# Attention weights times values with the values as TensorE's weights, in four column groups, and a way through HBM to put the result in order

## The chip, the cores and the metric

The kernel runs on one core of one Trainium2 chip. The metric is the device time of one execution in microseconds. A core has TensorE (matmuls, which write to PSUM), VectorE, ScalarE, GpSimd and SyncE; each runs its own queue in order and waits on semaphores. The profile names them PE (and PEld for TensorE's weight loads), DVE, ACT, POOL and SP.

## The reference

The input x has 16 sequences of 256 tokens of 128 numbers, all in fp32. It is one layer with an attention branch and a branch of experts on the same normalised input:

```python
xn = layernorm(x)
x = x + attn(xn) + ffn(xn)
# attn: h = layernorm(xn)*g1+b1; 16 query heads, 4 key/value heads, head size 8, rope
scores = where((col <= row) & (row - col < 32), q @ k.T / sqrt(8), -1e9)
out = softmax(scores) @ v                # the part that is changed
x1 = xn + out @ Wo + bo
attn = x1 + gelu(layernorm(x1) @ Wf1 + bf1) @ Wf2 + bf2
# ffn: 8 experts of 448 hidden units, the best two for each of the 4096 tokens
y = sum_e gate_e * (silu(x @ w1_e.T) * (x @ w3_e.T)) @ w2_e.T
```

## The kernel before

**Stages.** First x is normalised, q, k, v and the gate scores are computed for all tokens, and each (token, expert) pair gets a slot, so that 72 tiles of 128 slots each hold rows of a single expert. Then come 12 steps (k = 0 to 11), each with 6 expert tiles and parts of the attention of four neighbouring batches. Steps 3 to 10 are two-step bodies of a hardware loop; all others are written out. Steps 12 to 18 have no expert tiles: there the attention of the last batches is finished, and the feed-forward part of the attention branch (`up`, `down`), the sum of the experts' results and the stores of the output run. This is called the tail.

**An expert tile.** POOL gathers 128 rows of xn by an indirect DMA. TensorE transposes them (`transpose_xs`), VectorE copies them out (`take_xsT`), TensorE makes 7 products (`up_products`), ScalarE applies silu, VectorE multiplies (`gated`), TensorE makes 4 products (`down_product`), ScalarE takes the result out and POOL scatters it to HBM. A `down_product` waits for the copy `take_xsT` of the next tile, since both use one PSUM bank. SP loads the weights of a tile (448 KB) three tiles ahead, as soon as the products of the tile that used the buffer are done.

**Attention of batch b.** A batch has 256 queries in 8 blocks of 32. In its scores, partitions hold (key/value head, query in the block) and columns (head of the group, key). Because the window is 32 wide, the 32 columns of a query's own block and those of the block before can share one set of 32: for each query a key position is either in its own block or in the older one. `older_scores` and `own_scores` make both, `shift` takes one or the other and subtracts the maximum, `exps` takes exponentials and `weights_T` transposes. So `pT[:, n]` holds (head, key) by (g, query) for block n, and `pO[:, n]` the part of it that belongs to the own block. `vbd` holds the values of a block, block-diagonal over the four key/value heads, with four columns of ones behind (36 columns), and `dv` the difference to the block before. The result is the sum of pT with the older values and pO with the difference.

**The product that is changed** is `attend`, in four quarters of two blocks. `pT[:, n]` or `pO[:, n]` (128 columns) are the weights and `vbd` or `dv` (36 columns) move; block 0 has one product, each other block two, 15 in all. The result of block n stands in `turn_bank` with (g, query) in partitions and (head, d) and the four sums in columns. `norm` takes reciprocals of 32 sums, multiplies 256 columns, and one VectorE transpose in blocks of 32x32 makes `outT`, whose rows are features and columns tokens, as `project` (the product with Wo) needs it.

**Order of work around it.** Step k has, on TensorE: own scores of k, `heads` of k+1, tile, older scores of k, tile, own scores of k, tile, older scores, `transpose_h2` of k-3, tile (with quarter 0 of `attend(k-1)` ahead of the down product and quarter 1 behind it), tile (`project(k-2)` and quarter 2 ahead of the down product, quarter 3 behind it). In the tail no expert products stand between the quarters. `heads(b)` writes into `turn_bank`, and waits for `pv_normed` of batch b-3. VectorE does `norm(k-1)` as the last thing of step k, behind `residual(k-2)`. SP's queue has only weight loads in the steps, and in the tail loads of the experts' results and stores of the output, each behind waits for VectorE.

Of the kernel before, what the change touches and what calls it, by code (L numbers as in the profile page):

```python
# [22 lines left out]
P = 128  # L23
B, T, D = 16, 256, 128
NTOK = B * T
# [47 lines left out]
def layer(nc, x, wqkv, bqkv, wo, bo, g1, b1, g2, b2, wf1, bf1, wf2, bf2, gate, w13, w2,  # L73
          ident, cosf, sinf, older, newer, qmask, vmask, tri, rev, tilegrid, places, column, row, xn, ys, out):
# [4 lines left out]
    with ctx:  # L79
        def sb(name, shape, dt=F32):  # L80
            return ctx.enter_context(nc.sbuf_tensor(name, shape, dt))[:]

        def sem(name):
            return ctx.enter_context(nc.semaphore(name))
# [50 lines left out]
        def table(*shape):  # L135
# [103 lines left out]
        exp_ready, pT_ready, pv_psum, rsum_ready, pv_normed = (sem("exp_ready"), sem("pT_ready"), sem("pv_psum"),  # L239
                                                               sem("rsum_ready"), sem("pv_normed"))  # L240
# [34 lines left out]


# [21 lines left out]
        def _(sp):  # L298
# [160 lines left out]
        def _(dve):  # L459
# [245 lines left out]
            def norm(b):  # L705
                dve.wait_ge(pv_psum, b + 1)
                pv = turn_bank[:, 0:NBLK * VW].rearrange("p (n c) -> p n c", c=VW)
                nc.vector.reciprocal(rsum, pv[:, :, NKV * HD:VW]).then_inc(rsum_ready, 1)
                dve.wait_ge(rsum_ready, b + 1)
                nc.vector.tensor_tensor(  # L710
                    on.rearrange("p (n h d) -> p n h d", h=NKV, d=HD),
                    pv[:, :, 0:NKV * HD].rearrange("p n (h d) -> p n h d", d=HD),
                    bc(rsum.rearrange("p n (h a) -> p n h a", a=1), [P, NBLK, NKV, HD]), ALU.mult).then_inc(pv_normed, 1)
                dve.wait_ge(pv_normed, b + 1)
                nc.vector.transpose(outT, on).then_inc(outT_ready, 1)
# [311 lines left out]
        def _(pe):  # L1027
# [92 lines left out]
            def attend(b, p, quarter, h2T_out):  # L1120
                if quarter == 0:
                    pe.wait_ge(pO_ready, b + 1)
                    pe.wait_ge(dv_ready, b + 1)
                    if some(h2T_out):
                        pe.wait_ge(h2T_ready, h2T_out)
                for n in range(quarter * NBLK // 4, (quarter + 1) * NBLK // 4):
                    to = turn_bank[:, n * VW:(n + 1) * VW]
                    if n > 0:
                        nc.tensor.matmul(to, pT[:, n].rearrange("p g q -> p (g q)"), vbd[:, p, n, :], start=True, stop=False)  # L1129
                    last = nc.tensor.matmul(to, pO[:, n].rearrange("p g q -> p (g q)"), dv[:, p, n, :], start=(n == 0), stop=True)  # L1130
# [254 lines left out]
```

## Time and profile before

| | |
|---|---|
| median of 3 runs | 502.0 us (501.33 to 503.25) |
| profiled execution | 500.98 us, span 498.8 us |
| TensorE matmul busy | 437.2 us (88% of the span) |
| TensorE weight loads busy | 396.8 us (80%) |
| VectorE busy | 375.2 us (75%) |
| ScalarE busy | 254.9 us (51%) |
| GpSimd busy | 224.5 us (45%) |
| mean granted TensorE clock | 0.94 |
| moved by DMA | 57.21 MB |

The span runs from the first to the last instruction that the profiler recorded. Matmuls are pipelined and their ends are modelled, so the busy time of TensorE says less than the distance between the starts of neighbouring records. A share over the whole span is a mean over stages with different limits.

### The profile page before, as it was taken

What the parts mean: (1) busy time and instruction counts of PE and PEld (TensorE: products, weight loads), DVE (VectorE), ACT (ScalarE), POOL (GpSimd) and SP (SyncE); (2) the same over time, 40 slices, a digit from 0 to 9 for tenths busy, and PEclk for the clock granted to TensorE, in tenths of its full rate; (3) what the DMA queues carried; (4) which work ended last, traced back from release to release, by engine and by line L of the source; (5) the groups of instructions that cost most, each with busy time, mean ns of one, the idle gap of its engine ahead of it and who ended that gap; (6) DMA issues with size and microseconds to landing.
All of it is one profiled execution on the core that took longest, in us unless ns stands there. A gap on an engine that the chain in (4) does not pass through costs nothing. (4 is left out here: it accounts for less than half of the span.)

```text
span 498.8 us, 11145 instructions
## 1 busy us (share of the span) xinstructions
PE 437.2 (88%) x3310; PEld 396.8 (80%) x3311; DVE 375.2 (75%) x1010; ACT 254.9 (51%) x536; POOL 224.5 (45%) x252
## 2 busy tenths in 40 slices
PE   2943939879999999999999999989999999997996
PEld 2832539768989898989898989989999787785873
DVE  7947555857777777777777777777877979849874
ACT  2584244454645455555546465545545737553432
POOL 3630032546464656464646465555553841312320
PEclk9985558989999999999999999999999999999799
DMA  8950123424444545343444444433450600222211
GB/s 230 260 197 0 45 87 128 148 92 145 137 145 137 149 122 156 113 144 126 147 137 138 142 142 128 143 111 132 142 143 8 166 5 1 68 60 64 64 43 42
DMA packets 38033, 57.21 MB, mean 115 GB/s; under 512 B 6238, under 2 KB 25442, under 8 KB 37872
## 3 DMA queue, kind: packets, MB, share of 16 engines
q1 hardware_dynamic: 32528, 47.66, 31.5%
q0 software_dynamic: 4608, 8.93, 5.8%
q8 instruction: 18, 0.29, 0.2%
q10 hardware_dynamic: 864, 0.20, 0.2%
q14 instruction: 15, 0.12, 0.1%
HBM read 48.38 MB, written 8.91 MB: 115 GB/s over the span
## 5 line engine op out<-in xcount | busy, mean ns | idle before, releaser
L1166 PE MATMUL bank<-xsT,w_sb 128*128 128x128 f32 x1008 | 132.2, 284 | 16.1 <-DVE inter L761 10.8
L1166 PEld LDWEIGHTS bank<-xsT,w_sb 128*128 128x128 f32 x1008 | 121.0, 195 | 21.9 <-issue 18.4
L409 POOL DMA_INDIRECT scratch_ys<-ysb,pair x72 | 77.1, 1071 | 124.0 <-ACT ysb L953 114.5
L402 POOL DMA_INDIRECT xsb<-scratch_xn,token x72 | 73.8, 1026 | 59.7 <-DVE token L593 35.4
L1179 PE MATMUL bank<-w_sb,inter 128*128 x576 | 79.6, 281 | 4.1 <-issue 3.3
L1179 PEld LDWEIGHTS bank<-w_sb,inter 128*128 128x128 f32 x576 | 69.9, 191 | 7.6 <-issue 7.3
L953 ACT ACTIVATE ysb<-bank 128x128 f32<-128x128 f32 x72 | 19.8, 275 | 82.7 <-PE bank L1179 79.6
L759 DVE TENSOR_TENSOR inter<-bank,act 64x128 f32<-64x128 f32 x72 | 21.2, 295 | 38.2 <-ACT act L947 32.5
L1130 PE MATMUL bank<-dv,pO 128*128 128x36 f32 x256 | 49.3, 276 | 0.6 <-ACT h2T_sb L907 0.6
L1130 PEld LDWEIGHTS bank<-dv,pO 128*128 128x128 f32 x256 | 39.6, 194 | 2.7 <-issue 2.7
L761 DVE TENSOR_TENSOR inter<-bank,act 128x384 f32<-128x384 f32 x72 | 40.2, 558 | 1.0
L1129 PE MATMUL bank<-vbd,pT 128*128 128x36 f32 x224 | 40.8, 266 | 0.0
L750 DVE COPY xsT<-bank 128x128 f32<-128x128 f32 x72 | 20.7, 288 | 25.4 <-PE bank L1155 23.6
L946 ACT ACTIVATE act<-bank 64x128 f32<-64x128 f32 x72 | 19.4, 269 | 33.2 <-PE bank L1166 19.7
L947 ACT ACTIVATE act<-bank 128x384 f32<-128x384 f32 x72 | 35.4, 491 | 0.8
L930 ACT ACTIVATE S<-bank 128x512 f32<-128x512 f32 x32 | 19.5, 610 | 31.3 <-DVE pT L695 25.3
L1095 PE MATMUL bank<-kT,qbd 128*128 128x128 f32 x256 | 34.8, 280 | 0.7 <-ACT S L930 0.7
L1193 PE MATMUL bank<-h2T_sb,wf_sb 128*128 128x512 f32 x64 | 32.4, 631 | 2.3 <-ACT h2T_sb L907 1.3
L1129 PEld LDWEIGHTS bank<-vbd,pT 128*128 128x128 f32 x224 | 34.1, 192 | 0.0
L1108 PE MATMUL bank<-kT,qbd 128*128 128x128 f32 x224 | 31.5, 281 | 2.8 <-DVE S L682 2.8
L1204 PE MATMUL bank<-wf_sb,gT_sb 128*128 128x128 f32 x256 | 33.3, 293 | 0.8 <-ACT gT_sb L962 0.8
L1095 PEld LDWEIGHTS bank<-kT,qbd 128*128 128x128 f32 x256 | 32.1, 196 | 2.0 <-issue 1.1
(154 smaller groups left out, 810.0 us busy)
## 6 DMA issues: line engine op xcount, KB each, us to landing
w_sb<-in_w SPq DMA_DIRECT2D x72, 448.0 KB
w_sb<-scratch_ys SPq DMA_DIRECT2D x16, 256.0 KB, 3.3
scratch_xn<-xn_sb SPq DMA_DIRECT2D x8, 256.0 KB, 4.4
w_sb<-in_w SPq DMA_DIRECT2D x1, 2048.0 KB, 9.0
out_dram<-x_sb SPq DMA_DIRECT2D x8, 256.0 KB, 2.8
xsb<-scratch_xn,token POOLq DMA_INDIRECT x72
scratch_ys<-ysb,pair POOLq DMA_INDIRECT x72
x_sb<-in_x SPq DMA_DIRECT2D x3, 256.0 KB, 3.7
```

The costliest lines, as they stand in the source:

```text
L402: nc.gpsimd.indirect_dma_start(xsb[:, j % 3, :], None, xn, bass.IndirectOffsetOnAxis(ap=token[:, j:j + 1], axis=0)).then_inc(slots_in[j % ...
L409: nc.gpsimd.indirect_dma_start(ys, bass.IndirectOffsetOnAxis(ap=pair[:, j:j + 1], axis=0), ysb[:, j % 3, :], None, bounds_check=2 * NTOK - ...
L761: nc.vector.tensor_tensor(inter[:, p, 0:FULL], h3_bank[:, 0:FULL], act1[:, p, 0:FULL], ALU.mult).then_inc(inter_ready, 1)
L947: nc.scalar.activation(act1[:, p, 0:FULL], h1_bank[:, 0:FULL], ACT.Silu).then_inc(silu_ready, 1)
L1095: last = nc.tensor.matmul(bank[0][:, i * GW:(i + 1) * GW], qbd[:, p, n].rearrange("p h q -> p (h q)"), kT[:, p, :, (n + 1) * WIN:(n + 2) * ...
L1108: last = nc.tensor.matmul(bank[1][:, i * GW:(i + 1) * GW], qbd[:, p, n].rearrange("p h q -> p (h q)"), kT[:, p, :, n * WIN:(n + 1) * WIN], ...
L1129: nc.tensor.matmul(to, pT[:, n].rearrange("p g q -> p (g q)"), vbd[:, p, n, :], start=True, stop=False)
L1130: last = nc.tensor.matmul(to, pO[:, n].rearrange("p g q -> p (g q)"), dv[:, p, n, :], start=(n == 0), stop=True)
L1166: last = nc.tensor.matmul(to[:, c % EC * P:(c % EC + 1) * P], w13_sb[:, i % 3, c * P:(c + 1) * P], xsT[:, p, :], start=True, stop=True)
L1179: last = nc.tensor.matmul(y_bank[:, 0:D], inter[:, p, c * P:(c + 1) * P], w2_sb[:, ds(at + c * P, P)], start=(c == 0), stop=(c == EC - 1))
L1193: nc.tensor.matmul(bank[4 + c % 2], wf1_sb[:, c * P:(c + 1) * P], h2T_sb[:, i * 512:(i + 1) * 512], start=True, stop=True).then_inc(up_psu ...
L1204: last = nc.tensor.matmul(bank[6 + i % 2][:, t * D:(t + 1) * D], gT[i % 4][:, c, t * P:(t + 1) * P], wf2_sb[:, c, :], start=(c == 0), stop ...
```

## The change

For batches 0 to 14 the values become the weights (32 columns: four heads of 8), and the attention weights move (128 columns). The 32 result rows of block n = 4a + c go to partitions 32c to 32c+31, so that blocks c = 0 to 3 use the four column groups of the array. Quarters 0 and 2 make 8 such products (pT with the older values, then pO with the difference), quarters 1 and 3 make 4 products with `vmask_sb` as weights, which give the sums of the exponentials on the same rows as the results. In all there are 24 products for the 15 of before.

`norm` then takes reciprocals of 256 columns and multiplies; there is no transpose. The result `on` has (c, head, d) in partitions and (a, g, query) in columns. SP stores it to a scratch tensor in HBM and loads it again with four DMAs, one for each g, into `outT`, in runs of 32 numbers. These stand in SP's queue among the weight loads of step k = b+2 and, for the last batches, among the loads and stores of the tail. Batch 15 keeps the products, the narrow reciprocal and the transpose.

```diff
-        rsum = sb("rsum", [P, NBLK, NKV])
+        rsum = sb("rsum", [P, T])
...
+        def is_plain(b):
+            return isinstance(b, int) and b == B - 1
...
-            with sp.Fori(1, SLOT_TILES // 3) as n:
-                for p in range(3):
-                    load_weights(n, p)
+            def store_values(b):
+
+                sp.wait_ge(pv_normed, b + 1)
+                sp.dma_start(turned, on).then_inc(out_stored, 16)
+
+            def load_heads(b):
+
+                sp.wait_ge(out_stored, 16 * (b + 1))
+                for g in range(G):
+                    sp.dma_start(outT[g * 32:(g + 1) * 32, :].rearrange("x (a c q) -> x a c q", a=2, c=4),
+                                 turned.rearrange("(c x) (a g q) -> g x a c q", c=4, a=2, g=G)[g]).then_inc(outT_ready, 16)
+
+            def step(m, tiles=TILES):
+                for i in range(tiles):
+                    load_weights(2 * m + i // 3 + 1, i % 3)
+                    if i == 1 and exists(m - 2):
+                        store_values(m - 2)
+                    if i == 2 and exists(m - 2):
+                        load_heads(m - 2)
...
+            step(MSTEPS - 1, 3)
+            store_values(MSTEPS - 2)
+            load_heads(MSTEPS - 2)
...
+            regroup_first = {0: MSTEPS - 1, 1: MSTEPS, 2: MSTEPS + 1, 4: MSTEPS + 2}
             for i in range(GROUPS_A):
+                if i in regroup_first:
+                    store_values(regroup_first[i])
+                    load_heads(regroup_first[i])
                 sp.wait_ge(second_added, i + 1)
...
+                else:
+                    nc.vector.reciprocal(rsum, turn_bank[:, T:2 * T]).then_inc(rsum_ready, 1)
+                    dve.wait_ge(rsum_ready, b + 1)
+                    nc.vector.tensor_tensor(on, turn_bank[:, 0:T], rsum, ALU.mult).then_inc(pv_normed, 1)
...
+                else:
+                    a, total = quarter // 2, quarter % 2
+                    for i in range(1 if total else 2):
+                        for c in range(4):
+                            n = 4 * a + c
+                            to = turn_bank[32 * c:32 * c + 32, total * T + a * P:total * T + (a + 1) * P]
+                            weights = (pO if i else pT)[:, n].rearrange("p g q -> p (g q)")
+                            values = vmask_sb[:, 0:NKV * HD] if total else (dv if i else vbd)[:, p, n, 0:NKV * HD]
+                            last = nc.tensor.matmul(to, values, weights, start=(i == 0), stop=(i == 1 or total == 1))
...
-                pe.wait_ge(outT_ready, b + 1)
+                if is_plain(b):
+                    pe.wait_ge(last_turned, 1)
+                else:
+                    pe.wait_ge(outT_ready, 16 * G * (b + 1))
```

## Rows read from the trace of the kernel before

**Rows 1.** The page: busy time, share of the span, instructions of an engine

```profile
PE 437.2 (88%) x3310; PEld 396.8 (80%) x3311; DVE 375.2 (75%) x1010; ACT 254.9 (51%) x536; POOL 224.5 (45%) x252
```

**Rows 2.** Busy time in the window of one step; TensorE's longest wait, whole run

```profile
core 0: us, PE busy (x) PEld busy (x) DVE busy (x) ACT busy (x) POOL busy (x), PEclk, DMA share, GB/s
204.28:230.10 25.82, 24.75 (x214) 23.99 (x213) 19.97 (x52) 14.13 (x32) 14.72 (x16) 1.00 0.45 136
...
PE bank L1166 <- DVE inter L761: 10.8, 18, 2.3
```

**Rows 3.** TensorE's groups by shape: count, busy us, mean ns, idle before

```profile
L1129 PE MATMUL bank<-vbd,pT 128*128 128x36 f32 x224 | 40.8, 266 | 0.0
L1095 PE MATMUL bank<-kT,qbd 128*128 128x128 f32 x256 | 34.8, 280 | 0.7 <-ACT S L930 0.7
```

**Rows 4.** Timeline of TensorE in a step: start, length, records

```profile
222.62 0.31 PE L1130 MATMUL bank<-dv,pO 128*128 128x36 f32 x2
...
223.50 1.15 PE L1179 MATMUL bank<-w_sb,inter 128*128 x8
224.49 0.31 PE L1129 MATMUL bank<-vbd,pT 128*128 128x36 f32 x2
...
225.30 1.81 PE L1166 MATMUL bank<-xsT,w_sb 128*128 128x128 f32 x14
...
230.10 1.81 PE L1166 MATMUL bank<-xsT,w_sb 128*128 128x128 f32 x14
...
231.85 1.06 PE L1095 MATMUL bank<-kT,qbd 128*128 128x128 f32 x8
232.74 0.27 PE L1081 MATMUL bank<-ident_sb,qr 128*128 128x128 f32 x1
```

**Rows 5.** Timeline of VectorE in the same step and after it

```profile
223.08 0.28 DVE L750 COPY xsT<-bank 128x128 f32<-128x128 f32 x1
...
230.30 0.36 DVE L708 RECIPROCAL rsum<-bank 128x32 f32<-128x32 f32 x1 [0.17 <-PE bank L1130]
...
230.69 0.42 DVE L710 TENSOR_TENSOR on<-bank,rsum 128x256 f32<-128x256 f32 x1
...
232.05 0.29 DVE L750 COPY xsT<-bank 128x128 f32<-128x128 f32 x1 [0.45 <-PE bank L1155]
...
233.59 0.29 DVE L759 TENSOR_TENSOR inter<-bank,act 64x128 f32<-64x128 f32 x1 [1.25 <-ACT act L947]
```

**Rows 6.** VectorE's groups by shape, the whole run

```profile
L715 DVE STREAM_TRANSPOSE outT<-on 128x256 f32<-128x256 f32 x16 | 7.1, 445 | 0.5
...
L624 DVE RECIPROCAL mult<-mult 128x64 f32<-128x64 f32 x1 | 0.6, 553 | 0.0
```

**Rows 7.** Timeline of TensorE in the tail; brackets: idle before, and what ended it

```profile
415.25 1.16 PE L1108 MATMUL bank<-kT,qbd 128*128 128x128 f32 x8 [0.88 <-DVE S L682]
...
458.23 1.16 PE L1108 MATMUL bank<-kT,qbd 128*128 128x128 f32 x8 [1.97 <-DVE S L682]
...
474.70 0.31 PE L1130 MATMUL bank<-dv,pO 128*128 128x36 f32 x2
...
476.18 0.69 PE L1140 MATMUL bank<-wo_sb,outT 128*128 128x128 f32 x4
476.71 0.31 PE L1129 MATMUL bank<-vbd,pT 128*128 128x36 f32 x2
...
478.42 1.96 PE L1193 MATMUL bank<-h2T_sb,wf_sb 128*128 128x512 f32 x4
```

**Rows 8.** DMA issues: count, KB each, median us to landing; SP's queue in the tail

```profile
out_dram<-x_sb SPq DMA_DIRECT2D x8, 256.0 KB, 2.8
...
sin_sb<-in_sinf SPq DMA_DIRECT2D x1, 160.0 KB, 2.5
...
434.86 0.91 SPq L341 DMA_DIRECT2D w_sb<-scratch_ys  x2
```

**Rows 9.** Timeline of VectorE in the tail, norm of batch 14

```profile
466.88 0.36 DVE L708 RECIPROCAL rsum<-bank 128x32 f32<-128x32 f32 x1 [0.43 <-PE bank L1130]
```

More of the change, by code:

```diff
@@ L73, in layer @@
 def layer(nc, x, wqkv, bqkv, wo, bo, g1, b1, g2, b2, wf1, bf1, wf2, bf2, gate, w13, w2,
-          ident, cosf, sinf, older, newer, qmask, vmask, tri, rev, tilegrid, places, column, row, xn, ys, out):
+          ident, cosf, sinf, older, newer, qmask, vmask, tri, rev, tilegrid, places, column, row, xn, ys, turned, out):
     F32, F32R, BF16, I32 = mybir.dt.float32, mybir.dt.float32r, mybir.dt.bfloat16, mybir.dt.int32
@@ L327, in _ @@
                 load_weights(0, p)
-            with sp.Fori(1, SLOT_TILES // 3) as n:
-                for p in range(3):
-                    load_weights(n, p)
+            def store_values(b):
[13 more added lines that the diff above has]
+                        load_heads(m - 2)
+            step(0)
+            step(1)
+            step(2)
+            with sp.Fori(3, MSTEPS - 1) as m:
+                step(m)
+            step(MSTEPS - 1, 3)
+            store_values(MSTEPS - 2)
+            load_heads(MSTEPS - 2)
             ov = out.rearrange("(t p) d -> p t d", p=P)
@@ L706, in norm @@
                 dve.wait_ge(pv_psum, b + 1)
[L707 to L715, printed above, removed]
+                if is_plain(b):
+                    pv = turn_bank[:, 0:NBLK * VW].rearrange("p (n c) -> p n c", c=VW)
+                    sums = rsum[:, 0:NBLK * NKV].rearrange("p (n h) -> p n h", h=NKV)
+                    nc.vector.reciprocal(sums, pv[:, :, NKV * HD:VW]).then_inc(rsum_ready, 1)
+                    dve.wait_ge(rsum_ready, b + 1)
+                    nc.vector.tensor_tensor(
+                        on.rearrange("p (n h d) -> p n h d", h=NKV, d=HD),
+                        pv[:, :, 0:NKV * HD].rearrange("p n (h d) -> p n h d", d=HD),
+                        bc(sums.rearrange("p n (h a) -> p n h a", a=1), [P, NBLK, NKV, HD]), ALU.mult).then_inc(pv_normed, 1)
+                    dve.wait_ge(pv_normed, b + 1)
+                    nc.vector.transpose(outT, on).then_inc(last_turned, 1)
+                else:
+                    nc.vector.reciprocal(rsum, turn_bank[:, T:2 * T]).then_inc(rsum_ready, 1)
+                    dve.wait_ge(rsum_ready, b + 1)
+                    nc.vector.tensor_tensor(on, turn_bank[:, 0:T], rsum, ALU.mult).then_inc(pv_normed, 1)
             def residual(b):
@@ L1125, in attend @@
                         pe.wait_ge(h2T_ready, h2T_out)
[L1126 to L1130, printed above, removed]
+                if is_plain(b):
+                    for n in range(quarter * NBLK // 4, (quarter + 1) * NBLK // 4):
+                        to = turn_bank[:, n * VW:(n + 1) * VW]
+                        if n > 0:
+                            nc.tensor.matmul(to, pT[:, n].rearrange("p g q -> p (g q)"), vbd[:, p, n, :], start=True, stop=False)
+                        last = nc.tensor.matmul(to, pO[:, n].rearrange("p g q -> p (g q)"), dv[:, p, n, :], start=(n == 0), stop=True)
+                else:
[7 more added lines that the diff above has]
+                            last = nc.tensor.matmul(to, values, weights, start=(i == 0), stop=(i == 1 or total == 1))
                 if quarter == 3:
@@ L1378 @@
         aps[name] = nc.dram_tensor(f"in_{name}", a.shape, mybir.dt.from_np(a.dtype), kind="ExternalInput").ap()
-    for name, shape in (("xn", (NTOK, D)), ("ys", (2 * NTOK, D))):
+    for name, shape in (("xn", (NTOK, D)), ("ys", (2 * NTOK, D)), ("turned", (P, T))):
         aps[name] = nc.dram_tensor(f"scratch_{name}", shape, mybir.dt.float32, kind="Internal").ap()
```

5 lines of the change are left out of this document (3 added, 2 removed).

## The prediction

> **What bounds the kernel now.** I read the page's busy shares first: TensorE is busy 88% of the span and VectorE 75% [rows 1]. A share over the whole span hides stages, so next come the windows of whole steps. Between the routing at the start and the tail, in which no expert tiles are left, the kernel repeats one step of six expert tiles and one batch of attention. A step takes 25.82 us, and TensorE is busy 24.75 of it at a granted clock of 1.00 (2.4 GHz), VectorE only 19.97 [rows 2]. So inside a step TensorE's queue sets the pace, and a microsecond added to it is a microsecond of time. Its largest named wait over the whole run is 10.8 us for the gated product of VectorE, 18 times [rows 2]: VectorE is the engine that comes second, and it takes over as soon as TensorE gets much faster.
>
> Then the lines of the products that the change replaces. In this trace each fp32 matmul leaves two records. One with 36 moving columns has a mean of 266 ns, one with 128 moving columns 280 ns, and both have the full array as their tile, 128*128 [rows 3]. The timeline shows what they occupy: eight records with 128 moving columns (the own scores at 231.85) are followed by the next work 0.89 us later, 0.111 us per record; a quarter of the old attention product, eight records with 36 columns, goes from 224.49 to 225.30, 0.101 us per record [rows 4]. The short moving side saves nearly nothing, so it is the 128 columns of weights that fill the time. That is what the change goes for: it makes the values (32 columns) the weights and streams 128 columns.
>
> **TensorE's part.** Before, a batch has 15 products in four quarters (3, 4, 4, 4). In the step shown these take 0.67 us (six records at 0.111 from 222.62), then 0.81 us, and the two like it that follow 0.81 and 0.82: 3.11 us; behind the first quarter there are 0.21 us more until 223.50, where the down product waits for VectorE's copy of the next tile (223.08, 0.28 long) [rows 4, 5]. So 3.32 us stand in the step. After, a batch has 24 products: 16 with values as weights (8 blocks, two parts) and 8 with the mask as weights, which make the sums of the exponentials, broadcast over each head's rows. That is 48 records, each with 128 moving columns, so at 0.111 us each if nothing overlaps.
>
> Nothing in the trace shows two products side by side in different column groups, so I bound it. Below: four groups at once, 48/4 x 0.111 = 1.33 us. Above: none, 48 x 0.111 = 5.33 us. Between them: the two records of one fp32 product use the same column group and stand next to each other. If records start in the order of the program, the second has to wait for the first, and only it and the next product's first record can run together: one product per 0.111 us, 24 x 0.111 = 2.66 us. I take this value, because the timeline before shows records of one product following each other at the full 0.111, never closer.
>
> The Trainium skill (TensorE: Matmul & The Clock Gate, Part 3) says that matmuls start and end in strict program order and gives 2.38x for three column tiles, one record each. No run here shows it yet; by its order rule the pairing above holds, by its 2.38x alone the 48 records would be near 5.33 / 2.38 = 2.2 us, an estimate.
>
> Then the changes of array shape. In a step the four quarters are separated by expert products with 128-column weights, so the shape changes eight times per batch; in the tail quarters 0 and 1 stand together, as do 2 and 3, so four times. The trace has one shape only and no price for this. Bounds: nothing, if the pipeline runs through; and 0.280 - 0.111 = 0.17 us for the last record to end (its length less the spacing) plus 0.11 us for a weight load that can't go ahead, 0.28 us. I take 0.17 us, the part that every record of before shows as its overlap with the next [rows 3, 4].
>
> The Trainium skill (TensorEngine Tiling, Key Properties) has a rule against this change: changing the tiling mode drains TensorE. By that rule the price is above zero and the sum below stands; without it the sum would be the second rival's.
>
> Sum per step: 2.66 + 8 x 0.17 = 4.02 against 3.32, +0.70 us. Batches 0 to 10 are in the loop form: 11 x 0.70 = +7.7 us. In the tail a batch's products took 3.19 us (474.70 to 476.18 and 476.71 to 478.42, three more batches alike) [rows 7], after 2.66 + 4 x 0.17 = 3.34: +0.15, for batches 11 to 14 +0.6 us. Batch 15 is unchanged.
>
> **VectorE's part.** The reciprocal grows from 32 to 256 elements per partition. It costs more per element than other work of VectorE: 128x32 takes 0.36 us [rows 5] and 128x64 0.553 [rows 6], so 6.0 ns for each element more. That gives 0.36 + 224 x 0.0060 = 1.71 us; the lower bound is the 0.42 us of a 256-wide product [rows 5]. I take 1.71, since the two rows are of the same operation. The 0.45 us transpose [rows 6] goes, so a norm costs VectorE 1.71 - 0.36 - 0.45 = +0.90 us. In the loop this is hidden: right behind norm VectorE is idle 0.45 us before the copy at 232.05 and 1.25 us before the gated part at 233.59, which waits for ScalarE [rows 5]. What waits for norm is heads of the batch three later, at 232.74: reciprocal from 230.30, 1.71, a gap of 0.03 and the product's 0.42 end at 232.47, 0.27 us before [rows 4, 5]. If that cover were gone, up to 0.9 us a step would show.
>
> In the tail it isn't all hidden. VectorE runs without a pause from a norm to each of the two places where TensorE waits for it before its next scores, 0.88 us at 415.25 and 1.97 us at 458.23 [rows 7]. Each gets 0.90 later: +1.8 us. The other norms have idle time or expert sums behind them; I cost them at nothing, at most 0.9 us each for three.
>
> **The way through HBM.** One store of 128 KB and four loads of 32 KB with runs of 128 bytes replace the transpose. In the loop, store stands behind the second tile's weight load on SP's queue and the loads behind the third's; their consumer, project, comes three tiles later, at least 12 us (25.82 / 6 = 4.3 each). A 256 KB store landed in 2.8 us and a 160 KB load in 2.5 us, and two issues took SP 0.91 us [rows 8]. Behind them on SP are weight loads for tiles three later; 5 issues x 0.46 = 2.3 us of delay a step is covered by that distance. The closest place is batch 14: its norm begins at 466.88, the product would end 2.16 us later at 469.04, the store lands at 471.8, the fourth load starts 1.4 us on and lands at about 475.7, and project stood at 476.18 [rows 7, 8, 9]. Just hidden: zero. If small runs are slow, this once costs 1 to 4 us.
>
> **Sum.** 7.7 + 0.6 + 1.8 = +10.1 us. The profiled execution has a span of 498.8 us in 500.98 us; so 508.9 and 511.1. The median of the runs shown is 502.0, 1.0 above that execution: forecast 512 us.
>
> **Rivals.**
> A. Four groups really run side by side, with the same price of changing shape: 1.33 + 1.36 = 2.69 against 3.32, -0.63 x 11 = -6.9; tail (1.33 + 0.68 - 3.19) x 4 = -4.7; VectorE +1.8: -9.8, 492 us. For it: the output partitions are disjoint and the weights are small. Against: two records to a product, in order.
> B. Pairs, but changing shape is free: (2.66 - 3.32) x 11 = -7.3; tail -0.53 x 4 = -2.1; +1.8: -7.6, 494 us. This is the case on the other side, by one mechanism: at eight changes a step in the loop and four in the tail (104 in all) the point of no change is 7.6 / 104 = 0.07 us per change, well below the 0.17 I take. Against it: 0.07 is less than any gap that the trace shows for a pipeline that refills.
> C. The change doesn't do what it says: column groups run one after the other. 5.33 + 1.36 - 3.32 = 3.37 x 11 = +37; tail (5.33 + 0.68 - 3.19) x 4 = +11.3; +1.8: 552 us.
>
> **How the numbers follow.** Forecast's case 0.52, with prices of 0.10 to 0.28 us for a change of shape: 104 x 0.28 - 7.6 = +21.5 gives 523, 0.10 gives 505. A 0.16, B 0.14, C 0.10; 0.08 for a price near the point of balance. Measurements of this kernel spread over 0.4%, so 0.5% (2.5 us) is about what can be told from no change. Faster 0.30, same 0.08, slower 0.62. The range reaches to A and B below and to the forecast's upper price above, with C left out: 491 to 525; the forecast's own range is 505 to 523.
>
> **What would show it.** In the new profile: distance from the first attention record of a quarter to the next 128-column work (0.89 + 0.33 us for eight products, 0.44 + 0.33 for four); two products' records starting together or not; the gap before the first record of either shape (0.17); the reciprocal at 1.7 us; heads not waiting for the norm; project not waiting for a DMA, batch 14 above all; steps of 26.5 us. The prediction is wrong if products overlap fourfold, if shape changes cost under 0.07 us, or if nothing overlaps.

## The result and the profile after

The changed kernel takes 499.8 us (median of 7 runs, 496.9 to 499.8), the kernel before 501.9 beside it: a ratio of 0.9943, with a 95% interval of 0.9922 to 0.9964. It is 0.6% faster, 2.9 us by the ratio. The forecast was 512 us and slower. The profiled execution has a span of 498.0 us in 499.84 us, against 498.8 in 500.98 before.

**The products.** These are TensorE's groups of the changed lines by shape, in the profile after (count, busy us, mean ns of one, idle before), the answer to [rows 3].

```profile
L1178 PE MATMUL bank<-pT,vbd 128*32 128x128 f32 x240 | 12.8, 285 | 0.6 <-ACT h2T_sb L945 0.6
L1178 PE MATMUL bank<-pT,vmask_sb 128*32 128x128 f32 x240 | 12.6, 282 | 0.0
L1178 PE MATMUL bank<-pO,dv 128*32 128x128 f32 x240 | 12.1, 273 | 0.0
```

240 records of 285 ns would be 68 us if they stood one behind the other. Busy time counts each moment once, and is 12.8 us: so on average more than five of them lie over each other (a record is longer than its distance to the next, 0.28 us against 0.11 for one of the full array). The timeline of a step shows the distances, the answer to [rows 4].

```profile
223.56 0.27 PE L1206 MATMUL bank<-ident_sb,xsb 128*128 128x128 f32 x1
223.76 0.43 PE L1178 MATMUL bank<-pT,vbd 128*32 128x128 f32 x8
224.00 0.40 PE L1178 MATMUL bank<-pO,dv 128*32 128x128 f32 x8
224.34 1.16 PE L1230 MATMUL bank<-w_sb,inter 128*128 x8
225.42 0.42 PE L1178 MATMUL bank<-pT,vmask_sb 128*32 128x128 f32 x8
225.78 1.83 PE L1217 MATMUL bank<-xsT,w_sb 128*128 128x128 f32 x14
```

Eight records begin at 223.76 and the next eight at 224.00: 0.24 us for four products in four column groups, 0.030 us a record. That is two times 0.111, the time of one product's two records, for all four groups together. From the first of the 16 to the down product it is 0.58 us; the two eights take 0.24 and 0.22 us (the second distance is seen in quarters_together below), so 0.12 us lie behind the last. The eight records of the sums are followed by the next work after 0.36 us, again 0.24 + 0.12. Ahead of the first there are 0.09 us more than the transposition's 0.111 (223.56 to 223.76), and ahead of the sums 0.19 us more than the eight records' 0.89 (224.34 to 225.42). Each quarter so costs: 0.09 + 0.58 = 0.67 us, 0.19 + 0.36 = 0.55, then 0.68 and 0.55 in the second half. A batch has 2.45 us where it had 3.32, of which 0.21 were a wait for VectorE's copy that no longer shows.

**The rest of the step and of the run.** Windows of four steps in a row of the kernel after (us, busy times, granted clock, DMA share, GB/s) stand against [rows 2]. The third covers the same step as there.

```profile
155.27:180.72 25.45, 24.00 (x231) 21.86 (x230) 20.28 (x51) 14.33 (x33) 14.54 (x17) 1.00 0.55 151
180.72:206.96 26.24, 24.57 (x230) 22.01 (x230) 20.67 (x51) 14.38 (x34) 15.05 (x17) 1.00 0.52 146
206.96:232.78 25.82, 24.16 (x232) 21.96 (x230) 20.51 (x50) 13.85 (x32) 14.62 (x17) 1.00 0.51 145
232.78:257.74 24.96, 24.08 (x232) 21.88 (x230) 20.40 (x50) 14.43 (x34) 14.73 (x17) 1.00 0.57 153
```

TensorE is busy 24.0 to 24.6 us of 25 to 26, so 0.9 to 1.7 us of a step are pauses, where before they were 1.1. Nine steps, from `heads` at 128.73 to the one at 360.77, take 25.78 us each; before they took 25.94 (129.40 to 362.88). The attention products' place in a step became 0.87 us shorter, and the steps only 0.16. The tail, from there to the end of the span, grew from 135.9 to 137.2 us.

VectorE's norm, in its groups by shape and in the step (answers to [rows 5, 6]), and the place in the tail where TensorE waits for it:

```profile
L751 DVE RECIPROCAL rsum<-bank 128x256 f32<-128x256 f32 x15 | 26.2, 1744 | 1.9 <-PE bank L1178 1.4 <-issue 0.2
...
423.41 1.73 DVE L751 RECIPROCAL rsum<-bank 128x256 f32<-128x256 f32 x1
425.17 0.42 DVE L753 TENSOR_TENSOR on<-bank,rsum 128x256 f32<-128x256 f32 x1
...
425.70 0.45 PE L1119 MATMUL bank<-ident_sb,qr 128*128 128x128 f32 x1 [2.43 <-issue]
425.94 0.42 PE L1120 MATMUL bank<-ident_sb,kr 128*128 128x128 f32 x1
```

The name of this wait is "issue", but it ends 0.11 us after the product of the norm of batch 12 (425.17 + 0.42 = 425.59), for which `heads` of batch 15 has to wait. Behind it a single record lasts 0.42 us and the next comes 0.22 to 0.24 us later, instead of 0.27 and 0.11 in the loop: the granted clock has fallen from 2.4 to 1.2 GHz after 2.43 us without work. The window over these records shows it (0.50 of full speed; in the loop it was 1.00):

```profile
425.70:428.00 2.30, 2.30 (x8) 1.78 (x9) 2.27 (x4) 0.50 (x1) 2.15 (x2) 0.50 0.27 86
```

The way through HBM, SP's queue in the tail, with the last batch that uses it (14):

```profile
466.56 0.33 SPq L334 DMA_DIRECT2D scratch_turned<-on  x1
468.27 2.53 SPq L340 DMA_DIRECT2D outT<-scratch_turned  x4
...
474.86 0.69 PE L1191 MATMUL bank<-wo_sb,outT 128*128 128x128 f32 x4
```

The store is issued at 466.56 and the loads by 470.8, and `project` starts at 474.86 right behind the last product ahead of it (474.64), with no wait in the timeline. It is hidden here too. An issue of a load took SP 0.63 us (2.53 / 4), not 0.46.

### The profile page after: what moved, and what is told of

It is laid out like the page before. It is cut to its first block and busy times, and to the rows that moved or that the text cites. A ratio compares the mean times of both kernels' runs of the same rounds, so it can differ in the third digit from the quotient of the medians.

```text
span 498.0 us, 11704 instructions
## 1 busy us (share of the span) xinstructions
PE 423.9 (85%) x3580; PEld 363.7 (73%) x3581; DVE 386.5 (78%) x995; ACT 255.0 (51%) x536; POOL 226.4 (45%) x252
## 5 line engine op out<-in xcount | busy, mean ns | idle before, releaser
L1217 PE MATMUL bank<-xsT,w_sb 128*128 128x128 f32 x1008 | 132.6, 284 | 15.3 <-DVE inter L799 11.4
L441 POOL DMA_INDIRECT scratch_ys<-ysb,pair x72 | 81.1, 1126 | 119.6 <-ACT ysb L991 110.7
L1146 PE MATMUL bank<-kT,qbd 128*128 128x128 f32 x224 | 32.7, 287 | 6.1 <-DVE S L714 3.7
L1133 PE MATMUL bank<-kT,qbd 128*128 128x128 f32 x256 | 35.0, 280 | 1.8 <-ACT S L968 1.8
L1244 PE MATMUL bank<-h2T_sb,wf_sb 128*128 128x512 f32 x64 | 33.8, 653 | 2.5 <-ACT h2T_sb L945 1.3
L1146 PEld LDWEIGHTS bank<-kT,qbd 128*128 128x128 f32 x224 | 28.5, 196 | 9.8 <-issue 5.6
L1133 PEld LDWEIGHTS bank<-kT,qbd 128*128 128x128 f32 x256 | 31.9, 195 | 3.6 <-ACT S L968 1.9
L423 POOL TENSOR_TENSOR ve<-mv,eps_sb 128x2 f32<-128x2 f32 x16 | 4.7, 294 | 64.0 <-DVE mv L769 63.9
L1255 PE MATMUL bank<-wf_sb,gT_sb 128*128 128x128 f32 x256 | 30.4, 277 | 0.8 <-ACT gT_sb L1000 0.8
L1255 PEld LDWEIGHTS bank<-wf_sb,gT_sb 128*128 128x128 f32 x256 | 29.2, 192 | 2.4 <-ACT gT_sb L1000 1.6
L1000 ACT ACTIVATE gT_sb<-bank,cols_sb 128x512 f32<-128x512 f32 x32 | 21.2, 692 | 18.5 <-PE bank L1244 18.4
```

What stands on the lines that cost most here:

```text
L441: nc.gpsimd.indirect_dma_start(ys, bass.IndirectOffsetOnAxis(ap=pair[:, j:j + 1], axis=0), ysb[:, j % 3, :], None, bounds_check=2 * NTOK - ...
L1000: nc.scalar.activation(gT[i % 4][:, c, :], bank[4 + c % 2], ACT.Gelu, bias=cols_sb[:, 4 + c:5 + c]).then_inc(gelu_ready, 1)
L1133: last = nc.tensor.matmul(bank[0][:, i * GW:(i + 1) * GW], qbd[:, p, n].rearrange("p h q -> p (h q)"), kT[:, p, :, (n + 1) * WIN:(n + 2) * ...
L1146: last = nc.tensor.matmul(bank[1][:, i * GW:(i + 1) * GW], qbd[:, p, n].rearrange("p h q -> p (h q)"), kT[:, p, :, n * WIN:(n + 1) * WIN], ...
L1217: last = nc.tensor.matmul(to[:, c % EC * P:(c % EC + 1) * P], w13_sb[:, i % 3, c * P:(c + 1) * P], xsT[:, p, :], start=True, stop=True)
L1244: nc.tensor.matmul(bank[4 + c % 2], wf1_sb[:, c * P:(c + 1) * P], h2T_sb[:, i * 512:(i + 1) * 512], start=True, stop=True).then_inc(up_psu ...
```

## The experiments

The products became cheaper and the kernel hardly faster. Theory 1: the loads in short runs hold up the scatters and gathers of the expert tiles, so the DMAs give TensorE's gain back. Theory 2: the long reciprocal gives it back, mostly in the tail, where VectorE has no pause. A third came out of the first series. The kernel before took 502.7, 490.4, 490.6, 490.3 and 499.7 us in the five series, each on another chip, so a ratio is read only against the kernel before of the same series.

### Series 1: parts of the change taken away

**no_way** leaves out the way through HBM; `project` reads `on`, so its operand isn't in order.

```diff
-                sp.wait_ge(pv_normed, b + 1)
-                sp.dma_start(turned, on).then_inc(out_stored, 16)
-                sp.wait_ge(out_stored, 16 * (b + 1))
-                for g in range(G):
-                    sp.dma_start(outT[g * 32:(g + 1) * 32, :]
...
-                    pe.wait_ge(outT_ready, 16 * G * (b + 1))
+                    pe.wait_ge(pv_normed, b + 1)
...
-                    last = nc.tensor.matmul(vp_bank[:, T + t * P:T + (t + 1) * P], outT[:, t * P:(t + 1) * P], wo_sb,
+                    last = nc.tensor.matmul(vp_bank[:, T + t * P:T + (t + 1) * P], (outT if is_plain(b) else on)[:, t * P:(t + 1) * P], wo_sb,
```

> The changed kernel without the store to HBM and the four loads back; project takes the result as norm leaves it, so that the order of features and tokens is not put right (that part is left out). Median of the changed kernel 499.75 us. Theory 1 (the loads in short runs hold up the expert tiles' scatters and gathers, seen as ScalarE's copy of y waiting 2.85 us for a DMA behind the loads): 11 steps gain 0.4 to 0.5 us each, 494 to 496 us. Theory 2 (the long reciprocal of VectorE alone takes the gain back): within 1 us of 499.75.

498.5 us, ratio 0.9932 (0.9907 to 0.9956). Beside the change's 0.9943 (the change itself was not run in this series) this is no difference: by the two intervals the DMAs cost at most some 0.4%.

**narrow** takes the reciprocal of 32 columns only and multiplies all 256 by those; the other 224 reciprocals are left out.

```diff
-                    nc.vector.reciprocal(rsum, turn_bank[:, T:2 * T]).then_inc(rsum_ready, 1)
+                    nc.vector.reciprocal(rsum[:, 0:32], turn_bank[:, T:T + 32]).then_inc(rsum_ready, 1)
...
```

> The changed kernel with the reciprocal over 32 columns instead of 256, spread over the product by a broadcast (the normalisation is thereby left out for the other columns). Theory 2 (the reciprocal takes the gain back, mostly in the tail where VectorE has no pause): norm is 1.39 us shorter, tail gains 3 to 5 us, 494 to 497 us. Theory 1 (DMA): within 1.5 us of 499.75.

492.8 us, 0.9825 (0.9778 to 0.9872), 1.2% below the change, and more than theory 2 expected.

**no_way_narrow** is both edits.

> Both left out, the way through HBM and the long reciprocal (the order and part of the normalisation are left out). What remains is TensorE's own gain. If each step gives the 0.87 us that the distances in the profile show and the tail 1.1 us a batch: 502 - 9.6 - 4.4 = 488 us. If a third thing holds the steps (the gated product of VectorE behind ScalarE's silu), it stays above 492 us.

490.2 us, 0.9782 (0.9748 to 0.9817). Beside narrow this is no clear difference either: the two intervals overlap.

**old_with_way** has the products, narrow reciprocal and transpose of before for all batches; the store and the four loads go to a spare tile `beside`, and `project` waits for them too.

```diff
-            return isinstance(b, int) and b == B - 1
+            return True
...
-                    sp.dma_start(outT[g * 32:(g + 1) * 32, :].rearrange("x (a c q) -> x a c q", a=2, c=4),
+                    sp.dma_start(beside[g * 32:(g + 1) * 32, :].rearrange("x (a c q) -> x a c q", a=2, c=4),
...
+                pe.wait_ge(last_turned, b + 1)
...
```

> The kernel before with its old products, narrow reciprocal and transpose, and the store and four loads of each batch beside them into a spare tile; project waits for them as in the changed kernel. Theory 1: the DMAs cost 0.4 us a step by themselves, 506 to 508 us. Theory 2: 502 to 503 us.

498.5 us, 0.9938 (0.9918 to 0.9959). This was not what either theory said: work added to the kernel before, and it is as fast as the change. So on a chip of this kind a ratio of that size needs no new products. A part of it is TensorE's clock, which is not the same in every execution: the kernel before took 499.4 to 500.9 us in the 6 runs of this series with a mean granted clock of 0.944 or more and 502.0 to 504.2 in the 11 with 0.939 or less, and old_with_way has 10 of its 12 runs at 0.944 or more. The medians at that clock are 498.4 and 500.1 us, 0.35% apart instead of 0.62%. Two groups, in the window 129 to 363 us, show a difference, first the kernel before, then old_with_way:

```profile
L687 DVE TENSOR_TENSOR S<-S,rmax 128x512 f32<-128x512 f32 x18 | 14.9, 830 | 0.6
L418 POOL TENSOR_TENSOR xn_sb<-xn_sb,bo_sb 128x256 f32<-128x256 f32 x9 | 10.7, 1190 | 0.0
```

```profile
L720 DVE TENSOR_TENSOR S<-S,rmax 128x512 f32<-128x512 f32 x18 | 12.5, 692 | 0.6
L451 POOL TENSOR_TENSOR xn_sb<-xn_sb,bo_sb 128x256 f32<-128x256 f32 x9 | 7.1, 785 | 0.0
```

The timeline of the kernel before shows why the same operations take longer there: they run at the same time.

```profile
247.92 1.00 DVE L687 TENSOR_TENSOR S<-S,rmax 128x512 f32<-128x512 f32 x1
...
248.31 1.31 POOL L418 TENSOR_TENSOR xn_sb<-xn_sb,bo_sb 128x256 f32<-128x256 f32 x1
```

Theory 3: VectorE's subtraction in `shift` and GpSimd's `add_bo` slow each other where they meet (0.69 to 1.00, 0.76 to 1.31 us), and a kernel that moves one of them away from the other gains. The Trainium skill (GPSIMD Engine Reference, Specifications) says that GpSimd shares its SBUF interfaces with VectorE and contends with instructions that have two SBUF inputs; the two rows agree. The means of the other kernels of this series are 713 and 833 ns (the change), 809 and 1122 (no_way), 699 and 784 (narrow), 826 and 1191 (no_way_narrow). That already speaks against it as the whole answer: no_way_narrow meets as often as the kernel before, and is the fastest.

### Series 2: the two kept apart

**old_apart** and **new_apart** are the kernels before and after with one wait in GpSimd's queue, so that `add_bo` of step k follows the subtraction:

```diff
-            def add_bo(b):
+            def add_bo(b, k=None):
...
+                if exists(k):
+                    pool.wait_ge(shifted, 2 * k + 2)
...
```

> The kernel before, where GpSimd's addition of bo waits until VectorE has shifted the second half of the step's scores. Theory 3 (in the kernel before these two run at the same time and slow each other: the subtraction has a mean of 830 ns against 692 ns in old_with_way, the addition 1190 against 785, and the down product behind quarter 0 waits for it): 0.3 to 0.45 us a step in about 12 steps, 3.5 to 5 us faster than before, 497.5 to 499.5 us. If the order of SP's queue or the DMAs themselves made old_with_way faster: 501.5 to 503 us.

> The changed kernel with the same wait of GpSimd. Theory 3: the changed kernel has the collision only in part (subtraction 713 ns, addition 833 ns on the mean), so it gains little, 498.5 to 500 us, and is no faster than the kernel before with the wait. If the change itself were worth the 0.57%, it would stay 2 to 3 us below old_apart.

494.9 us, 1.0117 (1.0089 to 1.0146), and 493.6 us, 1.0067 (1.0042 to 1.0093), against 490.4 for the kernel before. Both were slower. Their means are 692 and 750 ns, but so they are in the kernels without the wait on this chip (old_queue below, 692 and 749), so there was nothing to win. In the tail the wait holds back GpSimd until 409.10; its additions then run beside VectorE's rotation of q and k, whose operations take 1.38 us there instead of 0.32, and the norm, and with it `heads`, come late (timeline of old_apart):

```profile
411.93 1.38 DVE L648 TENSOR_TENSOR rb<-qkb,sin_sb 128x160 f32<-128x160 f32 x1
...
420.53 0.30 PE L1083 MATMUL bank<-ident_sb,qr 128*128 128x128 f32 x1 [3.72 <-DVE on L712]
```

**old_queue** is the kernel before with SP's queue written out as in the change, and none of its DMAs.

> The kernel before with SP's queue written as in the changed kernel (three written-out steps, a loop of six tiles), without store and loads, nothing else changed. Theory 3: the collision is as before, since no DMA shifts GpSimd's scatters: 501 to 503 us. If the queue's form made old_with_way faster: 498 to 499 us.

490.9 us, 1.0004 (0.9987 to 1.0021): the form of the queue is worth nothing.

**log_exp** makes the reciprocal of the change on ScalarE, as exp(-ln(x)), behind the silu of the step's fifth tile.

```diff
-                    nc.vector.reciprocal(rsum, turn_bank[:, T:2 * T]).then_inc(rsum_ready, 1)
...
+                nc.scalar.activation(rsum, turn_bank[:, T:2 * T], ACT.Ln).then_inc(ln_ready, 1)
...
+                nc.scalar.activation(rsum, rsum, ACT.Exp, scale=-1.0).then_inc(rsum_ready, 1)
...
```

> The changed kernel with the 256-wide reciprocal of VectorE replaced by two activations of ScalarE, exp(-ln(sum)), right behind the exponentials of the scores. Theory 2 (VectorE's 1.74 us reciprocal takes back TensorE's gain; narrow measured 492.8): 493 to 496 us if ScalarE's tables hold both functions; if each needs a table load of 1.28 us, the next silu comes 2 us later and the gain is lost: 499 to 503 us.

518.5 us, 1.0579 (1.0559 to 1.0599). The two operations are short (384 and 416 ns), but ahead of each stands a load of ScalarE's function table, 1283 ns, 15 for either (the kernel after has none at this place). VectorE's product waits for them 54.8 us in the run, the longest 4.9 (ScalarE's groups, VectorE's wait):

```profile
L977 ACT ACT_TABLE_LOAD x15 | 19.2, 1283 | 0.3
...
DVE on L753 <- ACT rsum L979: 54.8, 14, 4.9
```

The time is above both ranges of the expectation. This says where not to put the work, and nothing on the theories.

### Series 3: the change and its parts on a third chip

**new_again** is the change; **old_loop_apart** and **new_loop_apart** have the wait of series 2 outside the tail only; **new_in_loop_only** is the change with the old products, narrow reciprocal and transpose for batches 11 to 15:

```diff
-            return isinstance(b, int) and b == B - 1
+            return isinstance(b, int) and b >= MSTEPS - 1
...
-            regroup_first = {0: MSTEPS - 1, 1: MSTEPS, 2: MSTEPS + 1, 4: MSTEPS + 2}
+            regroup_first = {}
```

> The changed kernel once more, beside kernels that tell its parts apart, since the kernel before took 502.7 us in the first series of experiments and 490.4 in the second. If the gain of 0.57% was a collision of VectorE and GpSimd that only the kernel before has: ratio 0.994 where the kernel before takes 502, and 1.000 to 1.012 where it takes 490. If it is the change's own: 0.994 in both.

> The kernel before with GpSimd's wait for the shifted scores in the steps with expert tiles only. Theory 3: 3.5 to 5 us faster than before where before takes 502; where it takes 490, within 1.5 us of it, since there is no collision to take away (in the second series the wait in the tail cost the 4 us).

> The changed kernel with the same wait. Steps of 24.4 us as in new_apart against 25.0 of the kernel before without a collision: 0.5 us x 11 = 5.5 us faster in the loop; in the tail the norm's 1.74 us reciprocal gives back 2 to 5 us. 1 to 4 us below old_loop_apart.

> The changed kernel with the old products, the narrow reciprocal and the transpose for batches 11 to 15, so that the tail is as before. Theory 2 (VectorE has no pause in the tail, and heads waited 2.43 us for the norm in the trace of the changed kernel): 1.5 to 4 us faster than new_again. If the tail's loss is the DMAs' or a matter of the clock: within 1 us of it.

| kernel | us | ratio (95%) |
|---|---|---|
| before | 490.6 | 1 |
| new_again | 485.9 | 0.9919 (0.9885 to 0.9953) |
| old_loop_apart | 490.0 | 0.9981 (0.9963 to 0.9999) |
| new_loop_apart | 484.7 | 0.9875 (0.9853 to 0.9897) |
| new_in_loop_only | 484.0 | 0.9853 (0.983 to 0.9876) |

new_loop_apart is 5.3 us below old_loop_apart, more than the 1 to 4 expected. The means of the two operations are 692 ns and 748 to 754 ns without the wait as with it: no meeting on this chip, so the series can't test theory 3, and the gain that is left here is not a collision's. Here the steps show what the change does to TensorE. These are windows of one step each, of old_queue (the kernel before's products, series 2) and of new_again (us, busy times of PE, PEld, DVE, ACT, POOL, then clock, DMA share, GB/s):

```profile
229.57:254.57 25.00, 24.61 (x214) 23.95 (x212) 19.59 (x51) 14.22 (x33) 14.22 (x17) 1.00 0.48 142
```

```profile
226.88:251.35 24.47, 24.08 (x232) 21.88 (x230) 20.56 (x50) 14.45 (x34) 14.43 (x17) 1.00 0.54 156
```

TensorE pauses only 0.4 us in either; it is the bound, and what it saves comes out. Over the seven steps from 154.58 to 330.11 the old products take 25.08 us a step, over those from 154.19 to 324.49 the new take 24.33: -0.75. The tails are 134.9 us (355.10 to 490.0) and 135.3 us (348.72 to 484.0). Windows of both tails, old_queue first:

```profile
355.10:490.00 134.90, 123.42 (x847) 103.38 (x845) 106.68 (x263) 65.61 (x114) 44.28 (x54) 0.96 0.21 61
```

```profile
348.72:484.00 135.28, 116.33 (x937) 90.96 (x935) 111.39 (x259) 65.73 (x114) 44.71 (x54) 0.96 0.27 73
```

TensorE is busy 7.1 us less, VectorE 4.7 us more (about five norms at 0.90), and the tail isn't shorter. TensorE's waits in these two windows show where it went, old_queue first (total, times, longest):

```profile
PE bank L1142 <- DVE S L710: 2.9, 2, 2.0
PE bank L1151 <- issue: 0.5, 2, 0.3
```

```profile
PE bank L1146 <- DVE S L714: 3.7, 2, 2.0
PE bank L1155 <- issue: 3.7, 2, 2.3
PE bank L1119 <- issue: 2.4, 1, 2.4
```

The wait for the scores' shift grew by 0.8 us, the one of `transpose_h2` (L1151, L1155) by 3.2, and that of `heads` (L1119) is new. new_in_loop_only, which gives up the new products there, is 0.7% faster than new_again by the ratios (with their intervals 0.2 to 1.1%).

### Series 4: the disputed costs by themselves

**group_by_group** has the two products of a column group next to each other, all else as in the change:

```diff
-                    for i in range(1 if total else 2):
-                        for c in range(4):
+                    for c in range(4):
+                        for i in range(1 if total else 2):
```

> The changed kernel with quarters 0 and 2 in another order: both products of a column group, then the next group, so that four records in a row use the same group. If records start in the order of the program (the step of the prediction that gave 0.111 us per product), the eight products take 0.9 us instead of 0.46 and a step 0.8 us more: 9 us slower than the changed kernel. If each group works off its own records, the eight products still take 0.46 to 0.55 us: within 1.5 us of it.

485.9 us, 0.9902 (0.9868 to 0.9936), as new_again. If a record could not start before all those ahead of it in the program, group 0's four would have to be through before group 1's first, and little would overlap. The timeline shows the 16 records in the same time:

```profile
168.73 0.45 PE L1178 MATMUL bank<-pT,vbd 128*32 128x128 f32 x8
168.97 0.42 PE L1178 MATMUL bank<-pO,dv 128*32 128x128 f32 x8
169.32 0.94 PE L1230 MATMUL bank<-w_sb,inter 128*128 x6
```

The eight records of four groups' first products come before the eight of the second ones, although the program alternates them. one_group below has the same order in the program, and there the records do alternate, so it is not the view that sorts them. The Trainium skill (TensorE: Matmul & The Clock Gate, Part 3) says strict program order in start and end; for starts in different column groups this timeline does not agree, and the measurement decides.

**one_group** sends every product to partitions 0 to 31, in that same order. The results of four blocks fall on top of each other, so they are not kept apart.

```diff
-                            to = turn_bank[32 * c:32 * c + 32, total * T + a * P:total * T + (a + 1) * P]
+                            to = turn_bank[0:32, total * T + a * P:total * T + (a + 1) * P]
```

> The changed kernel with every product's result written to partitions 0 to 31, group by group, so that one column group does all (the result of three quarters of the blocks is left out). Nothing can overlap: 48 x 0.111 = 5.3 us a batch against 1.4: +3.9 us a step, 35 to 50 us slower than the changed kernel. If the four groups are not what makes the products short, the time stays.

533.9 us, 1.0889 (1.0851 to 1.0927). The timeline:

```profile
152.47 0.41 PE L1178 MATMUL bank<-pT,vbd 128*32 128x128 f32 x2
152.71 0.38 PE L1178 MATMUL bank<-pO,dv 128*32 128x128 f32 x2
152.93 0.38 PE L1178 MATMUL bank<-pT,vbd 128*32 128x128 f32 x2
...
154.33 1.16 PE L1230 MATMUL bank<-w_sb,inter 128*128 x8
155.42 1.06 PE L1178 MATMUL bank<-pT,vmask_sb 128*32 128x128 f32 x8
```

Two records take 0.22 us, 0.11 each: no overlap. A step has 28.06 us (187.16 to 215.22), 3.7 more than new_again's 24.33; 48 records at 0.111 instead of 0.030 would be 3.9. The four groups are the whole gain: 32 weight columns alone bring nothing.

**narrow_again** is narrow in a series in which TensorE is the bound.

> The kernel of narrow (reciprocal over 32 columns), where before takes 490 us if this series is like the last two. Theory 2: the reciprocal costs mostly in the tail, 3 to 5 us: 481.5 to 483.5 us, ratio 0.982 to 0.986. If it costs in every step too: below 480.

479.4 us, 0.9759 (0.9728 to 0.979). The nine steps from 129.36 to 348.09 take 24.30 us each, against 24.43 for new_again (128.83 to 348.72), and the tail 129.7 us against 135.3. Its window, and the wait of `heads` that is 2.43 us in new_again as in the kernel after:

```profile
348.09:477.80 129.71, 114.09 (x937) 90.07 (x935) 106.77 (x258) 65.63 (x114) 45.71 (x54) 0.99 0.28 76
...
408.37 0.30 PE L1120 MATMUL bank<-ident_sb,qr 128*128 128x128 f32 x1 [0.81 <-issue]
```

The long reciprocal costs 0.13 us a step in the loop and 5.6 us in the tail. There the mean clock is 0.99 of full speed instead of 0.96, so a part of the 5.6 is the clock: the tail of the kernel before has taken 134.9 us at 0.96 (old_queue) and 133.5 at 0.99 (old_loop_apart). Against the latter narrow_again's tail is 3.8 us shorter: the products' gain of the tail, and five transposes of 0.45 us, once the long reciprocal doesn't take it. In series 1 no_way has a tail of 136.8 us at 0.98 and no_way_narrow one of 130.8 at 0.99, 6.0 less.

**old_with_way_again** is old_with_way on this chip.

> The kernel of old_with_way. Theory 3 (the DMAs only moved GpSimd's work out of the collision): where the kernel before has none, the DMAs gain nothing, ratio 1.000 to 1.006. If the DMAs or the code around them help by themselves: 0.994 again.

491.1 us, 1.0013 (0.9996 to 1.0031). Where the two operations don't meet anyway (692 and 752 ns), the DMAs bring nothing and cost 0.3% at most. What old_with_way won in series 1 goes with that chip, and isn't a gain of the DMAs as such.

### Series 5: fewer changes of shape, and the best parts together

**quarters_together** puts quarter 1 right behind quarter 0 and 3 behind 2, so a step has four changes of shape, not eight. **best_of_both** is new_in_loop_only with the wait of new_loop_apart.

```diff
                     attend(k - 1, 1 - p, 0, k - 2)
+                    attend(k - 1, 1 - p, 1, k - 2)
                 tile_down(3)
-                if exists(k - 1):
-                    attend(k - 1, 1 - p, 1, k - 2)
...
```

> The changed kernel with quarter 1 right behind quarter 0 and 3 right behind 2, both ahead of their down products, so that the shape changes four times a step and not eight. If a change of shape costs 0.1 to 0.17 us on TensorE's path: 0.4 to 0.7 us a step, 4 to 7 us faster than the changed kernel (485.9 where before takes 490). But the down product then stands behind all 12 products: where VectorE waits for the next up products, some of it is lost. No change, or slower: the changes of shape are hidden, or the order matters more.

> New products for batches 0 to 10, old products in the tail, and GpSimd's addition of bo behind the shifted scores in the steps. Against new_in_loop_only (ratio 0.985): equal where there is no collision, 0.984 to 0.986; 3 us better where before takes 502.

496.6 us, 0.9957 (0.9934 to 0.998), and 495.4 us, 0.9917 (0.9892 to 0.9942), against 499.7. The 4 to 7 us expected of quarters_together are not there: its ratio is no better than the change's 0.9943, though that was taken on another chip. The timeline of quarters_together shows the price of shape that it saves:

```profile
220.70 0.43 PE L1178 MATMUL bank<-pT,vbd 128*32 128x128 f32 x8
220.94 0.40 PE L1178 MATMUL bank<-pO,dv 128*32 128x128 f32 x8
221.16 0.40 PE L1178 MATMUL bank<-pT,vmask_sb 128*32 128x128 f32 x8
221.49 1.16 PE L1230 MATMUL bank<-w_sb,inter 128*128 x8
```

From 220.70 to 221.49 are 0.79 us for all twelve products of a half, with the gap ahead some 0.9, where the change has 1.22. But the steps are 25.47 us on average (127.74 to 357.00), as best_of_both's 25.40 (128.96 to 357.58): on this chip steps are again over 25 us in both, although nothing meets (692 ns in both). What is late there stands in the waits of best_of_both, 129 to 345 us:

```profile
ACT ysb L993 <- remote: 8.3, 3, 2.8
```

ScalarE's copy of an expert's result waits up to 2.8 us for a DMA, by the code the scatter that still reads its buffer, and the next down product's bank comes late by that. In 129 to 363 us these waits are 3.1 us in the kernel before, 11.4 in the kernel after and 16.5 in quarters_together; new_in_loop_only, of series 3, has none. They don't come from the way through HBM: no_way has 10.9 us and no_way_narrow 8.3, old_with_way none. They go with the new products, on this kind of chip only. The scatter itself has a mean of 1150 ns in best_of_both and 1079 in new_in_loop_only.

## Why the prediction was wrong, point by point

The forecast was slower, 512 us, and its own range 505 to 523; the kernel is faster. That 499.8 us lies inside 491 to 525 says nothing for the forecast, since that range was drawn to take in rivals A and B.

1. **Product rate (the step that failed).** The prediction bounded the 48 records by 1.33 and 5.33 us and took 2.66, "if records start in the order of the program", so that only pairs overlap. They take 2 x (0.46 + 0.24) = 1.4 us, nearly the lower bound. group_by_group shows that the order in the program doesn't matter, one_group that without separate column groups there is no overlap. The rows on which it rested [rows 3, 4] show only products of the full array, which share all columns; they couldn't say anything on this. Nor is it the 128 weight columns that fill the time, as the prediction read from them: in one_group a record with 32 weight columns still takes 0.11 us.
2. **Change of shape.** 0.17 us taken, within 0 to 0.28. Measured 0.09 or 0.19 us going in and 0.12 going out: about right, (2.45 - 1.4) / 8 = 0.13. With it rival A's 2.69 us per batch was 2.45, and -0.63 us a step was -0.75 where TensorE was the bound.
3. **The reciprocal.** 1.71 us predicted, 1.74 measured; all but hidden in the loop as predicted (narrow_again's steps are 0.13 us shorter). In the tail 1.8 us was mis-sized. It counted two waits of TensorE for the scores' shift, which grew by 0.8 us together, and costed three norms at nothing; but VectorE was busy 4.7 us more, and the waits of `transpose_h2` grew by 3.2 us. The wait of `heads` for the norm of batch 12 (2.43 us, 0.81 with the narrow reciprocal) is new, and after it TensorE's clock falls. Taking the long reciprocal away brings 5.6 us, but that is 1.4 us a norm, where the prediction's term is the 0.90 left after the transpose: in that proportion 3.6 us of the 5.6, an estimate.
4. **The DMAs.** Zero, as predicted, batch 14's included: old_with_way_again 1.0013, no_way no different from the change. The terms were off and cancelled: issues took 0.63 us, not 0.46, and the first load could be issued 1.7 us after the store (466.56 to 468.27), not 2.8.
5. **The sum.** Rival A had the mechanism and said -9.8 us: -6.9 in the loop and -2.9 in the tail. The profiled spans of old_queue and new_again, on two chips of the 490 us kind, differ by -6.4 us ahead of the tail and +0.4 in it, -6.0 in all. So the loop came out nearly as A has it, and the tail 3.3 us worse (point 3). The ratios of series 3 and 4 say less, -4.0 (0.9919) and -4.8 us (0.9902); the profiled execution of old_queue, 492.2 us, is 1.3 above its median.
6. **That steps are bound by TensorE.** True where the kernel before takes 490 us (a pause of 0.4 us a step), only partly on the chip of the profile shown: 1.1 us a step of pauses [rows 2], which the prediction read as a fixed part. TensorE's saving turned into pauses of up to 1.7 us there. In the traces of that kind ScalarE waits for scatters, which are longer there. What sets their lateness is open; it is not the way through HBM (series 5). How much of the 0.6% of that chip is products, how much that `add_bo` and the subtraction meet less, and how much the clock, is not separated: old_with_way reached 0.9938 without any new product, and no_way_narrow won while they met. no_way, which meets nearly as often as the kernel before, has steps of 25.62 us (128.72 to 359.27) against 25.94, so an estimate for the products there is 0.3 us a step. The sizes of the collision are shown; that it is worth a share of the time is only argued. old_loop_apart, on a chip without it, can't tell.

## What to carry to other kernels

Products with 32 weight columns to different column groups overlap fully here, in both orders tried, even when each leaves two records: four of them in the time of one, plus about 0.13 us for each change of shape. Use them where TensorE is the bound, and keep the older form where VectorE is (here the tail), if the new one brings wide operations such as a reciprocal at 6 ns per element of a partition. A fraction of a percent on one chip can come from what two other engines do at the same moment, or from TensorE's clock, so run it on several chips before you explain it.

## What the hardware showed that was not expected

- A weight load of 32 columns has records of 107 to 110 ns, one of 128 columns 195.
- VectorE's and GpSimd's operations, each with two SBUF inputs, slow each other where they meet: 0.69 to 1.00 us and 0.76 to 1.31 us, and in the tail of old_apart an operation of 128x160 0.32 to 1.38 us.
- The same kernel takes 490 us on three chips and 500 to 503 on two.
- Four loads of 32 KB in runs of 128 bytes take SP 2.53 to 2.67 us to issue in the kernel after, 0.63 to 0.67 each, the 128 KB store in one piece per row 0.33 to 0.37.
